# Filler products on TensorE in the steps without expert tiles of a recurrent layer with routed experts

## The reference

```python
# attention branch: delta rule, 4 heads, keys of 128, values of 64
S_t = S_{t-1} + k_t (beta_t * (v_t - k_t^T S_{t-1}))^T ; o_t = q_t^T S_t
s = (rms_norm(o) * norm_w * silu(xn @ Wg)) @ Wo
# expert branch: 8 experts, each token goes to the one with the largest logit
h = square(relu(xn @ expert_fc[e]));  y = h @ expert_proj[e].T
# result
out = x + s * silu(y)
```

## Time and profile before

| what | value |
|---|---|
| time, median of 3 runs | 887.62 us (886.36 to 890.33) |
| the profiled execution's own time | 888.67 us |
| span of its profile | 886.8 us |
| mean granted TensorE clock | 0.934 |
| TensorE products, busy | 787.5 us (89%) |
| VectorE busy | 514.9 us (58%) |
| ScalarE busy | 348.0 us (39%) |
| GpSimd busy | 365.9 us (41%) |

### The profile page before, as it was taken

How to read it: one execution, slowest core, us unless ns; L and a number is a source line. 1 busy time by engine, 2 the same in 40 slices (tenths; PEclk the granted TensorE clock), 3 DMA queues, 4 the chain that set the end, 5 groups by cost and what they waited for, 6 DMA issues and landing times.

```text
span 886.8 us, 21906 instructions
## 1 busy us (share of the span) xinstructions
PE 787.5 (89%) x8834; PEld 654.5 (74%) x8834; DVE 514.9 (58%) x1141; ACT 348.0 (39%) x736; POOL 365.9 (41%) x381
## 2 busy tenths in 40 slices
PE   3866379999999999999999999999999999996543
PEld 1344358888888888888888888888888878784432
DVE  5323555555555656555555556565655766666757
ACT  4701123444444443544444444435434434342212
POOL 4438663434344334234333443342343252524435
PEclk9979679999999999999999999999999999996555
DMA  9962140442543433534424434335344232004732
GB/s 321 381 248 102 54 174 6 165 171 108 188 147 133 169 135 130 198 132 158 177 109 177 158 129 171 136 126 203 132 153 181 96 132 98 19 2 155 248 96 84
DMA packets 44964, 130.86 MB, mean 148 GB/s; under 512 B 4608, under 2 KB 26240, under 8 KB 34880
## 3 DMA queue, kind: packets, MB, share of 16 engines
q1 hardware_dynamic: 41312, 119.74, 37.7%
q0 software_dynamic: 3552, 9.72, 3.0%
HBM read 105.02 MB, written 23.89 MB: 145 GB/s over the span
## 4 chain that ended last, share of the span: by engine, by line
PE 82%; DVE 6%; POOL 5%; issue 4%; ACT 2%; DMA 1%; SPq 0%; DVEq 0%; POOLq 0%; ACTq 0%
PE bank L453 17%; PE bank L464 16%; PE bank L524 6%; PE bank L496 6%; PE bank L484 6%; PE bank L433 4%; PE bank L431 4%; PE bank L432 4%; PE bank L657 3%; POOL sorted_x_d L1614 3%; PE bank L558 3%; PE bank L578 3%; PE bank L568 2%; PE bank L378 2%; PE bank L506 1%
## 5 line engine op out<-in xcount | busy, mean ns | idle before, releaser
L453 PE MATMUL bank<-xsT,wts 128*128 128x128 f32 x1248 | 175.3, 282 | 0.0
L453 PEld LDWEIGHTS bank<-xsT,wts 128*128 128x128 f32 x1248 | 156.7, 192 | 17.8 <-issue 17.2
L464 PE MATMUL bank<-wts,hT 128*128 128x256 f32 x624 | 169.4, 390 | 0.0
L1270 DVE TENSOR_TENSOR Pm<-bank,lvl_mask 128x256 f16<-128x256 f32 x192 | 72.7, 419 | 128.2 <-PE bank L558 126.9
L464 PEld LDWEIGHTS bank<-wts,hT 128*128 128x128 f32 x624 | 106.2, 191 | 12.6 <-issue 5.3
L1281 DVE TENSOR_TENSOR M<-bank,M 128x256 f16<-128x256 f32 x192 | 74.0, 420 | 56.3 <-PE bank L568 54.4
L933 ACT CAST Z<-bank 128x256 f16<-128x256 f32 x192 | 63.0, 375 | 97.7 <-PE bank L578 97.1
L1674 POOL TENSOR_TENSOR XTl<-f_t,XTh 128x512 f16<-128x512 f32 x32 | 37.0, 1157 | 130.8 <-DVE XTh L1215 130.7
L1691 POOL TENSOR_TENSOR ImM<-ident,M 128x512 f32<-128x512 f16 x32 | 36.3, 1155 | 107.5 <-DVE M L1281 107.5
L496 PE MATMUL bank<-xt,wq_sb 128*128 128x128 f32 x512 | 66.8, 286 | 4.0 <-DVE qT16l L1220 4.0
L496 PEld LDWEIGHTS bank<-xt,wq_sb 128*128 128x128 f32 x512 | 64.2, 200 | 7.5 <-issue 6.9
(11 more groups left out here) (197 smaller groups left out, 1917.4 us busy)
## 6 DMA issues: line engine op xcount, KB each, us to landing
wts<-in_fc SPq DMA_DIRECT2D x39, 1024.0 KB, 5.0
wts<-in_pj SPq DMA_DIRECT2D x39, 1024.0 KB, 7.6
sorted_x_d<-wts SPq DMA_DIRECT2D x11, 514.0 KB, 13.2
xs<-sorted_x_d SPq DMA_DIRECT2D x39, 128.5 KB
x_all<-in_x SPq DMA_DIRECT2D x8, 512.0 KB, 7.2
xnT_d<-wts SPq DMA_DIRECT2D x4, 1024.0 KB, 14.1
wts<-y_d SPq DMA_DIRECT2D x4, 1024.0 KB, 11.6
wts<-in_x SPq DMA_DIRECT2D x8, 512.0 KB, 6.2
```

Source lines behind the costliest of these rows:

```text
L453: ins = pe.matmul(psum[bank[n]][:, (c % 4) * P:(c % 4 + 1) * P], fcw[r][:, k, c * P:(c + 1) * P], xsT[:, k, :], start=(k == 0), stop=(k == ...
L464: ins = pe.matmul(psum[bank[0]][:, 0:D], hT[:, c, :], pjw[r][:, c, :], start=(c == 0), stop=(c == HC - 1))
L1270: dve.tensor_tensor(h4(Pm, b).rearrange("p h (n c) -> p h n c", c=s), half4(b).rearrange("p h (n c) -> p h n c", c=s), mask, ALU.mult).the ...
```

## The change

A new function `run_on(n, part)` issues n products of the identity with itself, 128 columns each, into bank 7, when its second argument is true. No semaphore stands with them, and nothing reads what they write. Their group stands in the `else` list, that is, in the steps without tiles, behind a product group of TensorE: behind 6 groups of the front, 20 of the levels and 4 of the chain. So step -1 gets 6 x 8 products, step 0 26 x 8, step 15 24 x 8, and step 16 4 x 8. These are 60 groups with 480 products, each with a weight load of its own. Nothing else changes.

```diff
+                def run_on(n, part):
+
+                    for _ in range(n if part else 0):
+                        pe.matmul(psum[H_BANK[1]][:, 0:P], ident16[:], ident16[:], start=True, stop=True)
@@ the list for steps without tiles
                         KS()
+                        run_on(8, chain)
                         K(0)
                         K(1)
                         U()
+                        run_on(8, chain)
                         Q(0)
                         M0()
+                        run_on(8, levels)
                         L(0)
+                        run_on(8, levels)
                         Dm(0)
+                        run_on(8, levels)
                         O()
+                        run_on(8, chain)
                         T(0)
+                        run_on(8, levels)
                         L(1)
+                        run_on(8, levels)
                         Q(1)
                         Dm(1)
+                        run_on(8, levels)
                         dS()
+                        run_on(8, chain)
                         T(1)
+                        run_on(8, levels)
                         L(2)
+                        run_on(8, levels)
                         VG(0)
                         Dm(2)
+                        run_on(8, levels)
                         kT(0)
+                        run_on(8, front)
                         kT(1)
+                        run_on(8, front)
                         T(2)
+                        run_on(8, levels)
                         ogT_()
                         G(0)
+                        run_on(8, front)
                         VG(1)
                         L(3)
+                        run_on(8, levels)
                         PTm(0)
+                        run_on(8, front)
                         G(1)
+                        run_on(8, front)
                         Dm(3)
+                        run_on(8, levels)
                         wo()
                         T(3)
+                        run_on(8, levels)
                         PTm(1)
+                        run_on(8, front)
                         L(4)
+                        run_on(8, levels)
...
                         F()
+                        run_on(8, levels)
                         Zc()
```

## The result

The changed kernel takes 891.29 us (median of 20 runs, 889.67 to 894.82) against 888.05 for the kernel before: ratio 1.0036, interval (95%) 1.0026 to 1.0046, so 3.2 us slower. I had forecast 1.5 us faster, and the result lies outside my range of 883.0 to 889.8, also when the 3.2 us are put on the median that I started from (890.8).

What follows compares the result with a forecast made beforehand. TensorE, 99.5% busy at full clock from 137.5 to 800 us, passes on changes at both ends, where the deciding engine varies. Step 0 -0.95, step 15 +0.25, `wo` -0.8: -1.5 us, giving 886.1 us, range 883.0 to 889.8.

Steps and rivals of the forecast that it cites:

- `wo`: Step 15's long product group on the chain: -1.5 us at full clock, +0.65 at half; taken as -0.8.
- Price of a filler group: Eight filler products cost 0.86 us at half and 0.45 us at full clock, ahead of TensorE's next group.
- Step -1: Six groups at the front: 0 us, since GpSimd's sends decide until 102.2 us.
- 103.9 to 110.25: Step 0, where TensorE decides: two groups before `Q(1)`, +0.4 us, between -0.35 and +1.2.
- 116.41 to 122.9: Step 0: full clock kept, +0.45 us of work covered, so 0; +2.5 if the clock falls.
- rival 2: Fillers don't help the clock or come too late, and delay the next leg: +8.8 us, 896.4 us; chance 0.12.
- 122.9 to 133.9: Levels of step 0: `L(4)` pushed by 0.67, faster legs give back 0.5: -0.15 us, between +0.5 and -0.5.
- 134.2 to 137.4: End of step 0: gapless work at half clock would run at full clock, -1.2 us, between 0 and -1.6.
- Step 15 to `O`: Three groups push `O` by 1.06 us, part of `O` runs fast: +0.25, between -0.4 and +0.9.
- Behind `wo`, and step 16: The last part: 0 us, fillers hide in TensorE's waits at either clock, and no clock rise expected.
- the rule that I weighed: Leaving no long idle gap between bursts avoids clock drops; fillers would then hold full clock at both ends, sum -7.3 us.

Runs made afterwards that it cites:

- e6: The changed kernel, unchanged, measured again on another chip against the kernel before: ratio 1.0036, 3.2 us slower.
- e5: The kernel before, unchanged, sent as a control run of its own: ratio 0.9999 (0.9990 to 1.0009).
- e1: The changed kernel with fillers in steps -1 and 0 alone, against the kernel before: ratio 1.0014, +1.2 us.
- e13: The kernel of e1 again, in another group, against the kernel before: ratio 1.0018, +1.6 us.
- e15: Only the filler groups of step 0 ahead of `Dm(3)`, against the kernel before: ratio 1.0028, +2.5 us.
- e3: The changed kernel with two filler products of 512 columns for each eight of 128, against the kernel before: ratio 1.0048, +4.2 us.
- e9: The changed kernel without its five groups ahead of `O` in step 15, against the kernel before: ratio 1.0047, +4.2 us.
- e4: The changed kernel without groups behind `kT`, `G`, `PTm`, nor behind `T(2)`, `L(3)` in step 0, against the kernel before: ratio 1.0031, +2.75 us.
- e16: Only step 0's groups between level products, without those behind `T(2)` and `L(3)`, against the kernel before: ratio 1.0014, +1.2 us.
- e14: Only the six filler groups of step -1, against the kernel before: ratio 1.0050, +4.4 us.
- e8: Fillers only from the group behind `O` of step 15 on, and in step 16, against the kernel before: ratio 0.9989, -1.0 us.
- e18: The kernel of e14 plus 160 TensorE instructions in idle places ahead of step -1, against the kernel before: ratio 1.0004, +0.4 us.
- e11: Only the filler group behind `KS` of step 15, against the kernel before: ratio 0.9998, -0.2 us.
- e10: Only the groups behind `M0`, `L(0)` and `Dm(0)` of step 15, against the kernel before: ratio 1.0003, +0.3 us.
- e12: Fillers only behind `dS` of step 15 and what follows, and in step 16, against the kernel before: ratio 0.9986, -1.25 us.

## Why the prediction was wrong

What failed is the overlap. Filler groups that I took as covered or half hidden lay on the path in full, and the one large gain, `wo`, did not come. By parts of the span, with the forecast beside what two pairs of profiles show:

| part, us | forecast | after less before | e6 less e5 |
|---|---|---|---|
| up to `krn` of step 0 | 0 | +0.2 | +1.4 |
| `krn` to second `k16l` | +0.4 | +0.3 | -0.5 |
| second `k16l` to second `X32` | 0 | +1.8 | +0.8 |
| second `X32` to `Fr` | -0.15 | +0.5 | +0.7 |
| `Fr` to first relu | -1.2 | -1.4 | -0.2 |
| steps with tiles, to `Fr` of step 14 | 0 | 0 | 0 |
| `Fr` of step 14 to the squares of `O` | +0.25 | +1.0 | +1.7 |
| squares to the end of `wo` | -0.8 | +0.2 | +1.35 |
| behind `wo` | 0 | -0.8 | -0.4 |
| sum | -1.5 | +1.8 | +4.9 |

Neither pair adds to the 3.2 us of the medians: e5 is the fastest of its runs, and `krn` of step 0 starts anywhere from 101.4 to 103.3 us, with the least and the most both in kernels without fillers in step 0. In the table below `krn` is the first of its three instructions, `Fr` is VectorE's last part of the levels, the first relu is ScalarE's in the first expert tile, and the squares are ScalarE's of `O`:

| leg, us | this code unchanged | with its fillers |
|---|---|---|
| `krn` to `k16l` (step 0) | 10.22 to 10.24 | 9.77 to 11.37 |
| second `k16l` to second `X32` | 7.66 to 9.48 | 8.43, 8.44 (e1, e6, e13, e15), 8.30 (e3), 10.46 and 12.03 (after, e9); 6.20 (e4, e16) |
| second `X32` to `Pm` of `L(4)` | 2.53 to 3.85 | 3.39 to 3.96 |
| `Fr` to first relu | 7.03 to 8.18 | 6.80, 6.81 |
| `Fr` of step 14 to `M0` | 10.47 to 10.50; 11.11 (e14) | 10.86 to 11.00; 10.49 (e3) |
| `M0` to `O` (step 15) | 2.78, 2.79 | 3.67 to 3.94 |
| `O` to its squares | 3.28 to 3.53 | 2.43 to 3.59; 4.31, 4.38 (e8, e9: only the group behind `O`) |

**Price of a filler group**, 0.86 and 0.45 us: right, they are rows of the chain (0.85, 0.45).

**Step -1**, 0: right, shown by e18 (+0.4, from -0.4 to +1.2).

**103.9 to 110.25**, +0.4 between -0.35 and +1.2: right. The profiles show both ends, 0.46 less in e1 and e6, 0.9 to 1.1 more in e3, e4, e13, e15, e16, and 0.3 in the profile after.

**116.41 to 122.9**, 0: the step that failed. The 0.45 us that the fillers add to the work were "covered: VectorE's next part began at 123.74, just when `XTl` left GpSimd at 123.69". That next part was `X32`, and it waits for `G`, behind the fillers; `XTl` was no cover but a neighbour in time. The 0.85 us row that I read as waiting was a late release: `X32` was released 1.01 us after the last product of `G(1)` began. The price was too low besides. At full clock and without the five groups on the way the leg to the second `X32` is 6.20 us (e4, e16), with them 8.44: 2.24, or five times 0.45, all of it on the path. The clock brings 1.5 us here, the fillers take 2.25. In the profile after there came 2 us of late releases on top, as in that of e9; there are none in e1, e6 or e13. My rival 2 had the fillers' mechanism, at half clock and +2.5 us; the clock was full and they cost all the same.

**122.9 to 133.9**, -0.15: the push of `L(4)` by the groups behind `T(3)` and `PTm(1)` was sized at 0.67, less the legs' 0.5. It measured 0.89 (3.42 for 2.53 us), two groups of 0.45, and the legs gave back 0.2 (5.41 for 5.62 to the first `Fr`) against the profile of e5, 0.6 against the profile that I had. A term that was mis-sized.

**134.2 to 137.4**, -1.2: right against that profile (8.18 to 6.81, so -1.4), but by luck. The same code needed 7.03 us in four other profiles (e5, e8, e11, e14), where the half clock fell elsewhere. The gain is 0.2 to 1.4 us, by the execution that it is held against.

**Step 15 to `O`**, +0.25 between -0.4 and +0.9: the mechanism is shown by e10 (+1.15 ahead of `O`, -1.10 in it, +0.3 us in all). In the whole change it was +1.0 and +1.7: the clock rose 0.7 and 1.95 us after `O` began, in e10 0.4; the group behind `O`, which e10 lacks, holds the squares back (4.31 for 3.53 us in e8); and a fetch stood between the sends of step 15 (0.4 to 0.5 us).

**`wo`**, -0.8: wrong in size and in direction in the whole change, and the term furthest off (+1.35 in e6). `wo` started 0.7 us later against the squares and took 3.22 us for 3.76: +0.2. e12 shows that the gain is there (1.95 us, the 1.85 that I had worked out). It is lost when fillers stand ahead of `O` too: three profiles against five show it. The reason is open. In e6 the clock rises at 817.5, in `O`, and is back at half from 827.7 to 838.0, over `wo`. In e8, without the groups ahead of `O`, it rises at 815.5, behind `O`, and falls at 825.7, but is full again at 829.1, before `wo` at 831.4. Both falls come at the same place, a wait of TensorE that one filler group doesn't fill (e6):

```profile
829.06 0.40 PE L583 MATMUL bank<-ident,M 128*128 128x64 f16 x4 [3.02 <-DVE M L1316]
```

**Behind `wo`, and step 16**, 0: nearly right; the profile after gains 0.8 there, that of e6 0.4. The clock did rise there, against the forecast: from 838.9 to 852.6, 866.2 to 873.1 and 879.9 to 883.3 in the profile after.

Not settled are the cause of the late releases and the fall of the clock over `wo`. The clock stood at 1.00 from 108.5 to 808.2 in the profile after, through both places of step 0 where it had fallen. By the rule that I weighed, the Trainium skill's "TensorE: Matmul & The Clock Gate", section "Why this matters for your kernels", closed gaps keep it up; in step 0 the trace agrees. In steps 15 and 16, while TensorE still had work, it fell at 808.2, 832.1, 852.6 and 873.1, each time in an idle gap of 2.3 to 4.9 us that the fillers left or at most 1.4 us behind one, so nothing there speaks against the rule.

## What to carry to other kernels

Filler products can keep the clock up, and they delay the product behind them wherever it is ready before they end: put them only where a wait is longer than they are, and count each group as a link of the chain unless the wait that it fills is named and measured. Here leaving them out in steps -1 and 0 and ahead of `dS` in step 15 turned 3.2 us lost into 1.25 us won (e12). Added instructions also move the fetches of all later ones: when a change in one stage moves the time in another, pad it by idle instructions to a multiple of 256 (the number found here) and measure again before you explain it. Sizes taken from one profile of stretches where the clock varies should be read in several profiles first.

## What the runs showed of the hardware

A fetch of TensorE's instructions (one packet on queue q8) between an indirect DMA's issue and its landing made GpSimd's wait 0.2 to 2.1 us longer, 58 times of 58 when it stood 0.5 to 2.0 us behind the issue. 96 idle instructions ahead of everything cost 4.2 us, 256 with the fillers of step -1 nothing. That the fetch itself delays the landing is argued from the order of the records; the transfer's inside was not seen, and the sends account for only a part of the 4.2 us.

A VectorE copy in fp16 took longer beside GpSimd's `PTl`: the copy `M` of 128x512 took 0.28 us at its shortest and 3.12 us beside two `PTl` (2.27 us) in step 15 of e6, ending after them.

TensorE's release of VectorE came up to 5.1 us after the last product of `G` began (usual: 0.23) in steps -1 and 0, beside GpSimd's indirect sends, in all eight profiles of the slower level and in none of the twelve others, in the kernel before as in the changed one. The cause is not known.
